# Keys' rows of the later steps transposed on VectorE and turned through DRAM, and normalised one step sooner

## What is computed

```python
xn = _layernorm(x, axis=-1)
# attention, segments of SEG = 512 rows, DIL = 8, BLOCK_M = 64
qkv = jnp.einsum('bmd,ed->bme', x, Wqkv)          # x is xn here
q, k, v = (qkv[0] * scale, qkv[1], qkv[2])
k4 = k.reshape(B, H, S, SEG, hd)[:, :, :, ::DIL]
v4 = v.reshape(B, H, S, SEG, hd)[:, :, :, ::DIL]
scores = jnp.einsum('bhspd,bhskd->bhspk', q4, k4)
c = jnp.max(scores, axis=4, keepdims=True)        # over blocks of 64 queries
w = jnp.exp(scores - c)
den = jnp.sum(w, axis=-1) + 1e-10
out = einsum(w, v4) / den, then @ Wout.T
# feed-forward
h = relu(xn @ W1 + b1);  y = h @ W2 + b2
result = x + attention + y
```

## Time and profile before

| | |
|---|---|
| median of 3 runs | 1060.14 us (1059.68 to 1060.82) |
| profiled execution, its own time | 1064.19 us |
| its span in the trace | 1062.2 us |
| PE busy | 1042.0 us, 98% of the span |
| DVE, ACT, POOL busy | 837.7, 648.1, 623.2 us |
| granted TensorE clock | full speed, 2.4 GHz, in every slice |
| DMA packets | 151895, 214.14 MB, mean 202 GB/s |
| SP's queue | 72.4% of 16 DMA engines' span |

### The profile page before, as it was taken

The page is one execution under the profiler, slowest core; times in us unless marked ns, Lnnn a source line. Parts: engine busy times, 40 slices in busy tenths (PEclk is TensorE's granted clock), DMA queues, the critical chain, the costliest instruction groups (busy, mean ns, idle before and its releaser), DMA issues.

```text
span 1062.2 us, 19202 instructions
## 1 busy us (share of the span) xinstructions
PE 1042.0 (98%) x5397; PEld 809.4 (76%) x5397; DVE 837.7 (79%) x1464; ACT 648.1 (61%) x1081; POOL 623.2 (59%) x489
## 2 busy tenths in 40 slices
PE   5999999999999999999999999999999999999998
PEld 4677777777787777787777777777877777877777
DVE  7987888878877887888878888788888878887752
ACT  5656665666666566666666656666565665656663
POOL 6355665656556556555656656565665565556564
PEclk9999999999999999999999999999999999999999
DMA  5157877687877778777778776868777787767754
GB/s 193 35 151 217 222 212 210 180 230 205 240 211 200 207 204 230 219 216 204 205 216 226 221 199 183 236 197 244 211 196 206 204 231 212 212 176 217 196 145 148
DMA packets 151895, 214.14 MB, mean 202 GB/s; under 512 B 27072, under 2 KB 95808, under 8 KB 151872
## 3 DMA queue, kind: packets, MB, share of 16 engines
q1 hardware_dynamic: 151728, 213.73, 72.4%
q10 hardware_dynamic: 144, 0.13, 0.0%
HBM read 100.01 MB, written 58.20 MB: 149 GB/s over the span
## 4 chain that ended last, share of the span: by engine, by line
PE 87%; DVE 5%; DMA 4%; issue 2%; SPq 1%; ACT 1%; DVEq 0%; ACTq 0%
PE h_bank L1081 38%; PE y_bank L1081 37%; PE s_banks L1156 5%; PE misc L1260 3%; PE s_banks L1260 2%; PE misc L1081 2%; DVE xn L858 1%; DMA k_pack<-k_dram 1%; DVE s_max L875 1%; DMA w_exp<-w 1%; DMA xt_dram<-z 1%; DVE w_exp L881 1%; DMA xt_raw<-xt_dram 1%; SPq L371 1%; DVE q_lo L924 0%
## 5 line engine op out<-in xcount | busy, mean ns | idle before, releaser
L534 POOL TENSOR_TENSOR h_lo<-h_full,h_hi 128x512 fp32r<-128x512 f32 x256 | 337.6, 1320 | 378.9 <-ACT h_full L625 376.9
L631 ACT ACTIVATE w_exp<-w_exp 128x512 f32<-128x512 f32 x256 | 161.6, 633 | 247.8 <-DVE w_exp L881 245.9
L623 ACT ACTIVATE h_hi<-h_bank,b_cols 128x512 fp32r<-128x512 f32 x256 | 174.7, 682 | 68.2 <-PE h_bank L1081 61.7
L1081 PE MATMUL h_bank<-xt_hi,w_hi 128*128 128x512 f32 x512 | 206.6, 403 | 0.0
L1081 PE MATMUL h_bank<-xt_lo,w_hi 128*128 128x512 f32 x512 | 200.3, 391 | 0.0
L1081 PE MATMUL h_bank<-xt_hi,w_lo 128*128 128x512 f32 x512 | 199.6, 390 | 0.0
L1081 PE MATMUL y_bank<-h_hi,w_hi 128*128 128x512 f32 x496 | 193.5, 390 | 0.2 <-ACT w_exp L631 0.2
L1081 PE MATMUL y_bank<-h_hi,w_lo 128*128 128x512 f32 x496 | 193.1, 389 | 0.0
L1081 PE MATMUL y_bank<-h_lo,w_hi 128*128 128x512 f32 x496 | 193.1, 389 | 0.0
L875 DVE TENSOR_REDUCE s_max<-s_banks 128x8 f32<-128x512 f32 x252 | 169.3, 672 | 29.0 <-PE s_banks L1156 28.5
L881 DVE TENSOR_TENSOR w_exp<-s_banks,s_max 128x512 f32<-128x512 f32 x252 | 174.2, 691 | 10.9
(11 more groups left out here) (146 smaller groups left out, 1542.6 us busy)
## 6 DMA issues: line engine op xcount, KB each, us to landing
q_pack<-q_hi SPq DMA_DIRECT2D x240, 128.0 KB, 2.5
rden_rows<-rden_dram SPq DMA_DIRECT2D x128, 128.0 KB, 4.6
x_b<-x SPq DMA_DIRECT2D x32, 512.0 KB, 4.7
x_raw<-x SPq DMA_DIRECT2D x31, 512.0 KB, 4.9
yt_dram<-y_mem SPq DMA_DIRECT2D x124, 128.0 KB, 3.5
y_mem<-yt_dram SPq DMA_DIRECT2D x31, 512.0 KB, 4.5
out<-x_b SPq DMA_DIRECT2D x31, 512.0 KB, 3.1
q_pack<-q_lo SPq DMA_DIRECT2D x120, 128.0 KB, 2.4
```

The source lines that it names most:

```text
L534: pool.tensor_tensor(h_part[1][:, i % HBUF], h_full[:, i % HBUF], f32(h_part[0][:, i % HBUF]), ALU.subtract).then_inc(h_lo, 1)
L623: act.activation(h_part[0][:, i % HBUF], h_bank[i % 2][:], ACT.Relu, bias=b1_cols[:, i:i + 1]).then_inc(h_hi, 1)
L631: act.activation(w_exp[:, pair], w_exp[:, pair], ACT.Exp).then_inc(w_ready, 1)
L1081: mm = pe.matmul(ps, stationary[a], moving[b], start=start and c == 0 and n == 0, stop=stop and c == len(pairs) - 1 and n == 2, skip_group ...
```

## The change

The keys' rows of steps 2, 4, ... 28 (14 of them) are no longer transposed on PE. At the end of the odd step before, DVE normalises them and turns their 32x32 blocks into the first 256 columns of `z`. SP writes these with four DMAs to a new buffer `xk_dram`, in pieces of 32 numbers (128 bytes), and reads them back with one DMA of 128 KB into `xn_keys`, which holds them transposed from then on. ACT's `keys_hi` and DVE's `keys_lo` read `xn_keys` in place of the PSUM bank. POOL's `inverse_deviation` stands ahead of the two `hidden_lo` of the tail. Before step 1 nothing changes.

```diff
+        xk_dram = nc.dram_tensor("xk_dram", [D // PW, PW, P // PW, PW], F32).ap()
+        z_keys = z[:].rearrange("p j t n -> p (j t n)")[:, 0:D].rearrange("p (j n) -> p j n", n=PW)
...
+        def keys_transposed(s):
+            return key_banks(s)[0][:, 0:DH * P] if by_tensor(s) else xn_keys[:]
...
+            def key_blocks_to_dram(s):
+                sp.wait_ge(z_keys_ready, s + 1)
+                for i in range(P // PW):
+                    sp.dma_start(xk_dram[:, :, i].rearrange("j c n -> c j n"),
+                                 z_keys[PW * i:PW * (i + 1)]).then_inc(xk_out, 16)
+            def keys_in(s):
+                sp.wait_ge(xk_out, (s + 1) * 32)
+                sp.dma_start(xn_keys[:].rearrange("p (a k) -> p a k", a=DH),
+                             xk_dram.rearrange("(a j) c i n -> (j c) a (i n)", a=DH)).then_inc(xk_in, 16)
...
                     pack(s, 1)
+                if load and par == 1:
+                    key_blocks_to_dram(s)
                 if attention:
                     den_to_dram(s + 1)
...
                     den_spread(s + 1)
+                if load and par == 1:
+                    keys_in(s)
                 if norm:
                     pack(s, 3)
...                                     (POOL, end of a step)
+                if load:
+                    inverse_deviation(s + 3, 1 - par)
                 segment, tail = tail_tiles(s, attention)
                 for i in tail:
                     hidden_lo(segment, i)
-                if load:
-                    inverse_deviation(s + 3, 1 - par)
...                                     (ACT, keys_hi)
-                act.wait_ge(xkey_psum, s + 4)
+                if by_tensor(s):
+                    act.wait_ge(xkey_psum, s + 4)
+                else:
+                    act.wait_ge(xk_in, s * 8)
...                                     (DVE)
+            def transpose_key_blocks(s):
+                dve.wait_ge(xn_keys_ready, s + 2)
+                dve.transpose(z_keys, xn_keys[:].rearrange("p (j n) -> p j n", n=PW)).then_inc(z_keys_ready, 2)
+            def transpose_blocks(s, keys):
+                if keys:
+                    dve.wait_ge(xk_out, s * 32)
...
-                    if n == 0 and keys:
-                        normalise_keys(s + 2)
...
                 elif ffn:
+                    if load and par == 1:
+                        normalise_keys(s + 3)
+                        transpose_key_blocks(s + 3)
                     output_blocks(s)
...                                     (PE)
-                    if i == KEY_TILES[0] and norm and par == 0:
-                        transpose_keys(s)
```

More of the change, by code:

```diff
@@ L189, in ln_attention_ffn @@
         xt_in = sem("xt_in")
+        z_keys_ready = sem("z_keys_ready")
+        xk_out = sem("xk_out")
+        xk_in = sem("xk_in")
         xkey_psum = sem("xkey_psum")
@@ L645, in keys_hi @@
             def keys_hi(s):
-                act.wait_ge(xkey_psum, s + 4)
+                if by_tensor(s):
+                    act.wait_ge(xkey_psum, s + 4)
+                else:
+                    act.wait_ge(xk_in, s * 8)
                 act.wait_ge(kv_psum, past(s + 2))
-                act.copy(xkey[0][:].rearrange("p c k -> p (c k)"),
-                         key_banks(s)[0][:, 0:DH * P]).then_inc(xkey_hi, 2)
+                act.copy(xkey[0][:].rearrange("p c k -> p (c k)"), keys_transposed(s)).then_inc(xkey_hi, 2)
             def transposed_hi(s, par):
@@ L823, in normalise_keys @@
                 dve.wait_ge(rstd_ready, s + 1)
-                dve.wait_ge(xkey_psum, past(s))
+                if isinstance(s, int) and s <= 2:
+                    dve.wait_ge(xkey_psum, s)
+                else:
+                    dve.wait_ge(xkey_hi, s)
+                    dve.wait_ge(xkey_lo, s)
                 dve.tensor_scalar(xn_keys[:], x_keys[:], mean_var[:, T, 0:1], rstd[:, T:T + 1],
@@ L830, in keys_lo @@
                 dve.wait_ge(xkey_hi, s + 4)
-                dve.tensor_tensor(xkey[1][:].rearrange("p c k -> p (c k)"), key_banks(s)[0][:, 0:DH * P],
+                dve.tensor_tensor(xkey[1][:].rearrange("p c k -> p (c k)"), keys_transposed(s),
                                   f32(xkey[0][:]).rearrange("p c k -> p (c k)"),
@@ L862, in normalise @@
                 op.then_inc(xn_ready, 1)
-            def transpose_blocks(s):
+            def transpose_key_blocks(s):
[4 more added lines that the diff above has]
+                    dve.wait_ge(xk_out, s * 32)
                 dve.wait_ge(xn_ready, s + 3)
@@ L992, in step @@
                         normalise(s + 2, par)
-                        transpose_blocks(s)
+                        transpose_blocks(s, keys)
                     if n == KEY_TILES[0] - 2 and keys:
```

## The result

The changed kernel takes 1071.65 us, median of 6 runs (1068.3 to 1076.68). The kernel before, run on the same chip, takes 1060.68 (1059.68 to 1061.94). The ratio is 1.0107, 95% interval 1.0084 to 1.0131: 11 us slower, where 3 us faster was forecast, and above the end of the range. The profiled execution of after is its longest, 1076.68 us with a span of 1074.8, so its rows are used for what happens inside a step, and the medians for what the whole kernel costs.

The account below looks back on a forecast made before the run. PE, busy 98% of the span, was taken as the bound. From 1060.14, 3.6 us of transposes come off and 0.9 for late residuals is given back: 1057.4 us, own range 1055.1 to 1058.0, 8-in-10 range 1055.2 to 1063.2.

Parts of the forecast that it names:

- What is added on DVE and POOL, and what hides it: Odd step: statistics at 355.05, `rstd` near 356.65, normalisation from 356.9 taking 0.41, blocks at 357.75, under DVE's wait until 358.00.
- the slack of 0.5 to 0.6: Even step: `keys_lo` done at 367.6, PE needing it at 368.2; so 0.5 to 0.6 us spare.
- The transposes' worth: Even steps: two transposes take 0.26 us of PE's queue; 14 pairs removed give 3.6 us.
- The rival of the whole duration: The transposes' full time comes off PE, 28 x 0.271 = 7.6 us, giving 1052.5; chance 0.02.
- The block transpose: DVE, odd step: 256 columns take 0.45 us, from the line through 0.72 for 512 and 1.25 for 1024.
- `hidden_lo` not harmed, the output's blocks not late: Odd step: `rstd` ends before POOL's next work at 356.84; PE asks for the output's banks near 361, leaving 2 us.
- Four writes 1.86, read's landing 2.6, `keys_hi` 0.37, `keys_lo` 0.39: Keys' way over SP, ACT and DVE: times in us, with the read issued at 364.2 and `keys_lo` ending at 367.6.
- The rule on transfers under 512 bytes: Such transfers miss line rate; for the 128-byte writes SP's issue would go to the upper bound, as in the round-trip rival.
- The long round trip: SP's writes take 2.83, PE waits 0.47 in all 14 steps: 1063.1, or 1066.3 with a landing of 3.8; chance 0.20.
- The late residuals: Four odd steps with late `add_residual` stall PE, 5.5 us together, in timed runs too: 1060.6 to 1062.0; chance 0.12.

Follow-up runs that it names:

- e6: Changed kernel, with POOL's tail `hidden_lo` waiting for DVE's keys' normalisation and the keys' read issued ahead of the spread of the denominators: 1056.46 us.
- e10: e6, with POOL in even steps also waiting for `keys_lo` before `hidden_lo(3)` and doing the residual behind it: 1055.56 us.
- e8: Kernel before without the 14 transpose pairs, keys read untransposed from SBUF, POOL's `hidden_lo(3)` and residual put behind `keys_lo` in even steps: 1056.6 us.
- e5: Kernel before without the 14 transpose pairs, `keys_hi` and `keys_lo` still reading the PSUM bank with its left-over content: 1058.31 us.
- e7: e6, with DVE normalising and block-transposing the keys ahead of `add_residual` in odd steps: 1079.1 us.
- e4: Changed kernel, with the read of the transposed keys issued later, behind `pack(s, 3)`: 1122.23 us, ratio 1.0581.
- e9: Changed kernel, orders kept, with DVE's normalised keys written to a free PSUM bank and block-transposed from there: 1063.6 us, ratio 1.0045.

## Why the prediction was wrong

**The step that failed** is in "What is added on DVE and POOL, and what hides it": "DVE starts the normalisation 0.26 after `rstd` ... 356.9, and takes 0.41", together with the "1.4 us" for POOL's two operations. The normalisation was measured where POOL stood idle, POOL's pair where DVE had only a block transpose out of PSUM, and both were carried to a place where the other engine works on SBUF. The chain from statistics to written blocks was costed at 357.75 - 355.05 = 2.70 us. It measured 757.30 - 753.12 = 4.18. Of the 1.48 between, 0.81 is the normalisation (1.22 against 0.41), and nearly all of the rest POOL: 0.36 for `var_eps` (0.55 against 0.19) and 0.33 for `rstd` (1.51 against 1.18), beside `add_residual`.

The numbers for it stood in the same paragraph: `h_lo` "became ready at 356.84" and the normalisation was to start at 356.9. They were joined only to ask whether POOL would be late. The lengthening itself was in before's trace. DVE, three tiles of before (duration ns min/median/max):

```profile
L858 DVE TENSOR_SCALAR xn<-x_raw,mean_var,rstd x128: 401/406/2484, 9.8 to 980.5; 128x256 f32<-128x256 f32 x128
...
L920 DVE TENSOR_TENSOR k_lo<-k_full,k_hi x32: 407/1323/1325, 18.2 to 991.3; 128x256 fp32r<-128x256 f32 x32
...
L886 DVE TENSOR_SCALAR den<-den x32: 151/740/1590, 50.0 to 1036.4; 128x64 f32<-128x64 f32 x32
```

One operation, one shape, and a longest of 3, 6 and 10 times the shortest: that needs a cause outside the instruction. `k_lo` has the shape of `keys_lo`, two SBUF inputs and 1.32 us, where `keys_lo` with one PSUM input has 0.39.

**Where the lost time goes.** 1.5 late, of which the slack of 0.5 to 0.6 covers a third: by the prediction's own working 0.9 to 1.0 of stall per step. PE's wait is 14.8 / 14 = 1.06. Then 14.8 - 3.6 = 11.2, measured 11.0. That the two agree to 0.2 is partly luck: the 14.8 come from the longest of the runs, the distances give 14 x 0.93 = 13.0, and the two profiled executions differ by 1076.68 - 1064.19 = 12.5. So the account holds to some 2 us. Within that the slack, the number of steps and the worth of the transposes were right; one term decided the sign.

**Point by point.**
- *The transposes' worth, 0.26 per pair of steps*: right. e6 0.24, e10 0.26, where e8 and e5 show only 0.12 to 0.14; the four fastest kernels are 3.9 to 5.4 us below before. The rival of the whole duration (7.6 us) did not come. The 275 ns that the prediction takes from the Trainium skill ("TensorE: Matmul & The Clock Gate", Part 4) is given there for bf16; these transposes are float32.
- *The block transpose, 0.45 from the line through two wider ones*: 0.45 in all 14, and not lengthened by POOL.
- *`hidden_lo` not harmed, the output's blocks not late*: right for PE in after (`y_mem` starts at 757.22, PE was not kept waiting), though POOL's `h_lo` starts some 0.4 us later than forecast (755.31 - 753.12 = 2.19 behind the statistics, for 356.84 - 355.05 = 1.79). In e7 it was the other way.
- *Four writes 1.86, read's landing 2.6, `keys_hi` 0.37, `keys_lo` 0.39*: 1.79, 2.3, 0.40, 0.43. The writes start 0.02 after the blocks. The page of before has 27072 packets under 512 bytes, after 42528; 14336 of the new ones are the 56 writes of 32 KB in pieces of 128 bytes. The rule on transfers under 512 bytes ("DMA: Bandwidth & Descriptors", Specifications, in the Trainium skill) would have shown as a slow issue or a late landing, and neither is there: these writes land sooner than any in the earlier trace rows. After's DMA issues (KB each, median us to landing):

```profile
xk_dram<-z SPq DMA_DIRECT2D x56, 32.0 KB, 1.7
xn_keys<-xk_dram SPq DMA_DIRECT2D x14, 128.0 KB, 2.3
```

- *The long round trip* was the rival that came nearest: 14 steps of waiting ahead of `keys_values` did come. But its mechanism, on SP, was wrong (the writes took 1.79 us and the read landed in 2.3), and its time of 1063.1 to 1066.3 was too low. It had 0.20.
- *The late residuals* came in after's profiled execution too, less than in before: DVE's waits for `y_mem` are 9.6 us in 7 places, against 15.4 in 9. The prediction had their path right, from the late residual to a late `keys_lo`, but not that a late residual also meets `h_lo` and is lengthened by it. Two of them, DVE:

```profile
162.89 2.40 DVE L983 TENSOR_TENSOR x_b<-y_mem,x_b 128x512 f32<-128x512 f32 x2 [1.04 <-DMA y_mem<-yt_dram]
...
492.32 3.29 DVE L983 TENSOR_TENSOR x_b<-y_mem,x_b 128x512 f32<-128x512 f32 x2 [2.01 <-DMA y_mem<-yt_dram]
```

  They took 2.40 and 3.29 us in place of 1.26, and the waits ahead of `keys_values` behind them are the two longest, 1.85 and 1.74 us in place of 0.9. Three distances of this execution, 67.19, 66.80 and 67.04, are together 5.4 us longer than three of 65.2; they are those that end in these two waits, and the one behind the first. Behind the wait of 1.85 matmuls run at half pace, as in e4; behind the one of 1.74 they don't:

```profile
177.39 0.47 PE L1122 MATMUL misc<-wkv_hi,xkey_hi 128*128 128x512 f32 x1 [1.85 <-ACT xkey_hi L679]
...
180.32 0.63 PE L1122 MATMUL h_bank<-xt_hi,w_lo 128*128 128x512 f32 x1
```

Open: what makes `y_mem` late in single steps, and why the runs of one kernel differ (e9 by 12 us, after by 8, e8 by 6, e10 by 2), was not separated.

## What to carry to other kernels

A duration read from a trace belongs to the place where it was read. Before an instruction of VectorE with all operands in SBUF (two input tensors, or one that is scaled) is moved, look at what GpSimd does at the new place, and the other way round; if it works there, count its whole instruction as a wait. A group whose shortest and longest differ by a factor of three is where to look for such pairs, and the cure can be an operand in PSUM, or one wait that lets the short, urgent instruction go first.

## What the runs showed of the hardware

- The standstill is not a slowdown in proportion: 64 columns and 256 columns both end when POOL's instruction ends (1.25, 1.22, 1.32 us, where undisturbed they take 0.18, 0.41 and 0.38). In an undisturbed step DVE loses each time to the engine that it waits for: POOL makes `rstd` and goes on to its next instruction at once (0.03 before the end that the record gives for `rstd`), and DVE starts 0.2 later.
- Two long instructions on both sides hold each other up in turn: in e7 two `h_lo` took 2.99 us in place of 2.59, and the two halves of DVE's residual beside them 3.36 in place of 1.26.
- A wait of 2.85 us of PE was followed by some 3.5 us with matmuls at half pace (0.42 to 0.43 us between starts; e4), one of 1.85 by nearly as much (after), while those of 0.87 and 1.74 were not (after). So a late operand has a price in steps: the wait of 2.85 cost 4.6 us in all.
- Writes to DRAM in pieces of 128 bytes, 32 KB each, issued at 0.45 us each and landed in 1.7.
